# An expert's weights in one transfer instead of two, in a mixture-of-experts stage on one core

## The chip, the core and the metric

The kernel runs on one core of one Trainium2 chip. The metric is the time on the device in microseconds (us), from one execution to the next the median of three. A core has five engines with a queue of instructions each: TensorE (PE, with its weight loads shown apart as PEld), VectorE (DVE), ScalarE (ACT), GpSimd (POOL) and SyncE (SP), which here does nothing but start transfers. Transfers run on 16 DMA engines, and say by a semaphore that they have landed.

## What is computed

Two layers, each of a cross attention and a feed-forward part, on 800 tokens of width 1024. The change lies in the feed-forward part of layer 0, a mixture of 32 experts of which each token takes four:

```python
logits = x @ gate_w.T + gate_b
topk_logits, topk_idx = jax.lax.top_k(logits, 4)
topk_weight = softmax(topk_logits)
# rows sorted by expert (xt, gid: the expert of each row), then for each expert:
gate = xt @ w_gate[e] + b_gate[e]            # w_gate[e], w_up[e]: 1024 x 512
up   = xt @ w_up[e]   + b_up[e]
gate = minimum(gate, 7.0); up = clip(up, -7.0, 7.0)
activated = (up + 1.0) * gate * sigmoid(1.702 * gate)
outs = activated @ w_down[e] + b_down[e]     # w_down[e]: 512 x 1024
y = sum over the token's four experts of outs * topk_weight
```

All weights are float32. One expert has 4 MB of gate and up weights (1024 x 1024 numbers) and 2 MB of down weights (512 x 1024 numbers), 6 MB in all, beside a small bias row.

## The kernel before, in words

The stages run one after the other: attention 0, the mixture (`moe`), attention 1, a ternary feed-forward part. Each engine has its own program, and semaphores tie them.

**Blocks and steps.** The router counts how many rows each expert gets and rounds them up to blocks of 64 rows (`BS`). With the inputs of this kernel there are 67 blocks (the router's counts follow from the inputs). The list of blocks, in the order of the experts, is cut into three queues of 23 (`NQ_W` is 3), and the stage takes a block of each queue in turn, so that step `s` works on queue `s % 3`. A loop of 12 passes over six steps gives 72 steps.

**Weights.** SBUF holds three places for an expert's weights, one for each queue: `W2[:, q, :]`, of which the first `W2_D` = 8192 numbers of a partition are gate and up and the other 4096 are down, and `bias3[:, q, :]`. An expert stays in its place while its queue has blocks of it. When a queue goes on to its next expert, the place is loaded anew. There are 34 loads (`N_LOADS`): one for each queue at the start, and 31 in a loop on SP. The router's tables tell this loop, for load `i`, the expert, the place, and how many steps must be done before the place is free (`load_i`, rows 0, 1 and 2). By L1230 that last number is the first step of the new expert less two: the place is free when the step three before the first use is over, since that was the last one of its queue.

**One step of TensorE** (`one` in `moe_tensor`, L1467). It reads the table `need_g` for the number of loads that must have landed, waits for the semaphore `m_wg`, and runs the first half of the gate and up matmuls of step `s` (L1442), the transposes of the next tile of rows (`turn`, L1434) and of the activations of step `s - 1` (`turn_act`, L1450), the second half of gate and up, which signals `m_gu`, and last the down matmuls of step `s - 1` (`down`, L1463), which signal `m_y`. So the down part of a step is over only at the end of the step behind it. `down` reads a table of its own, `need_d`, and waits for a semaphore of its own, `m_wd`.

**One load on SP** (`moe_sync`, L1359 to L1373). Wait until the load before has landed (`m_wg`), and until the gate and up matmuls of the last step that used the place are over (`m_gu`): start the 4 MB of gate and up (L1365). Wait for that step's activations (`m_act`): start the two bias transfers (L1368), which count on `m_wg` too. Wait until the down part of the load before has landed (`m_wd`) and the last down matmuls of the place are over (`m_y`): start the 2 MB of down (L1372). SP works through this in order.

**The rest.** POOL gathers the next 128 rows of tokens into the one buffer `hs` (L1394), one gather for two steps, as soon as TensorE has transposed the rows before (`m_tp`). ACT empties the transposes and the results and starts the stores of the results `ysb` (L1554) from a queue of its own. DVE applies the activation (L1494 to L1502). The router's own buffers lie where the weights of places 1 and 2 will be: `pt` in the gate and up part of place 2, `pl` in the down part of place 2, which is in use until the last gate weights are in (`m_gk`).

Of the kernel before, what the change touches and what calls it, by code (L numbers as in the profile page):

```python
# [9 lines left out]
I32 = mybir.dt.int32  # L10
U32 = mybir.dt.uint32
ALU = mybir.AluOpType
# [4 lines left out]
P = 128  # L17
# [3 lines left out]
E, TOPK, FI = 32, 4, 512  # L21
# [19 lines left out]
G = 2  # L41
# [12 lines left out]
MAX_STEPS = IT * MAX_IT  # L54
# [1 line left out]
MIN_TILES = MIN_IT * TPI  # L56
FILL = -(-(MAX_TILES - MIN_TILES) // HG)
N_LOADS = E + NQ_W - 1
GU_INC, DN_INC = 16 * (1 + G), 16
assert MAX_STEPS <= P and N_LOADS <= P and T <= BS * MIN_BLOCKS // NQ_W  # L60
EC = FE // P
NBLK = 2
# [14 lines left out]
W2_D = KC * 2 * FI  # L77
W2_N = W2_D + IC * D
# [76 lines left out]
def build(nc, A, stages=("a0", "moe", "a1", "ffn")):  # L155
    ctx = ExitStack()
    with ctx:
        sems = {}

        def sem(name):  # L160
            if name not in sems:
                sems[name] = ctx.enter_context(nc.semaphore(name))
            return sems[name]
# [6 lines left out]
        PS = ctx.enter_context(nc.psum_tensor("PS", [P, 8, 512], F32))  # L170
# [85 lines left out]
        idxc = [pm.put(f"idxc{i}", [P, 1], I32) for i in range(TPI)]  # L256
        np_i = pm.put("np_i", [P, 4], I32)
        need_g = pm.put("need_g", [P, MAX_STEPS], I32)
        need_d = pm.put("need_d", [P, MAX_STEPS], I32)
        first_e = pm.put("first_e", [P, NQ_W], I32)  # L260
        load_i = pm.put("load_i", [P, 3, N_LOADS], I32)

# [867 lines left out]
        def route_vector(dve):  # L1130
# [113 lines left out]
            dve.sem_inc(sem("m_te"), 1)  # L1244
            dve.wait_ge(sem("m_tet"), 1)
            ts(need_g[0:1, :], PS[0:1, 1, 0:MAX_STEPS], float(GU_INC), float(GU_INC), ALU.mult, ALU.add)
            ts(need_d[0:1, :], PS[0:1, 1, 0:MAX_STEPS], float(DN_INC), float(DN_INC), ALU.mult, ALU.add)
            for k in range(3):
                vt.tensor_copy(load_i[0:1, k, :], PS[0:1, 1, (k + 1) * P:(k + 1) * P + N_LOADS])
            link(dve, ts(np_i[0:1, 0:1], rounds[0:1, :], 1.0, None, ALU.add))  # L1250
# [68 lines left out]

        def moe_sync(sp):  # L1320

            def load_gate_up(e, q):
                sp.dma_start(W2[:, q, 0:W2_D], A["W2"][e, :, 0:W2_D]).then_inc(sem("m_wg"), 16)

            def load_bias(e, q):
                for g in range(G):
                    sp.dma_start(bias3[g * BS:(g + 1) * BS, q, :],
                                 A["b2"][e, g:g + 1, :].to_broadcast([BS, N1])).then_inc(sem("m_wg"), 16)

            def load_down(e, q):  # L1330
                sp.dma_start(W2[:, q, W2_D:W2_N], A["W2"][e, :, W2_D:W2_N]).then_inc(sem("m_wd"), 16)

            sp.wait_ge(sem("a_qc"), 16 * HG)
            sp.wait_ge(sem("m_fill"), 16 * HG)
            load_gate_up(0, 0)
            load_down(0, 0)
            sp.wait_ge(sem("a_folded"), 2)
            sp.dma_start(gwT[:, :, :], A["gwT"].rearrange("p (c e) -> p c e", c=KC)).then_inc(sem("m_gw"), 16)
            sp.dma_start(gb[:, :], A["gb"].to_broadcast([P, E])).then_inc(sem("m_gw"), 16)
            sp.dma_start(bd, A["bd"]).then_inc(sem("m_gw"), 16)  # L1340
            load_bias(0, 0)
            for m in range(MT):
                sp.wait_ge(sem("ln_hn"), ln_count("moe", "hn", m + 1))
                sp.dma_start(h_d[m * P:(m + 1) * P, :], HN["moe"][m % 2][:, :]).then_inc(sem(f"moe_st{m % 2}"), 16)
            sp.wait_ge(sem("m_first"), 1)
            sp.wait_ge(sem("moe_st0"), 16 * ((MT + 1) // 2))
            sp.wait_ge(sem("moe_st1"), 16 * (MT // 2))
            for q in range(1, NQ_W):
                if q == 2:
                    sp.wait_ge(sem("m_tab"), 1)  # L1350
                e = sp.value_load(first_e[0:1, q:q + 1], min_val=0, max_val=E - 1)
                sp.wait_ge(sem("m_wg"), GU_INC * q)
                load_gate_up(e, q)
                load_bias(e, q)
                if q == 2:
                    sp.wait_ge(sem("m_gk"), TOPK)
                sp.wait_ge(sem("m_wd"), DN_INC * q)
                load_down(e, q)
            with sp.Fori(NQ_W, N_LOADS) as i:  # L1359
                e = sp.value_load(load_i[0:1, 0, bass.ds(i, 1)], min_val=0, max_val=E - 1)  # L1360
                q = sp.value_load(load_i[0:1, 1, bass.ds(i, 1)], min_val=0, max_val=NQ_W - 1)
                done = sp.value_load(load_i[0:1, 2, bass.ds(i, 1)], min_val=1, max_val=MAX_STEPS)
                sp.wait_ge(sem("m_wg"), GU_INC * i)
                sp.wait_ge(sem("m_gu"), done)
                sp.dma_start(W2[:, bass.ds(q, 1), 0:W2_D].rearrange("p a n -> p (a n)"), A["W2"][e, :, 0:W2_D]).then_inc(sem("m_wg"), 16)  # L1365
                sp.wait_ge(sem("m_act"), done)
                for g in range(G):
                    sp.dma_start(bias3[g * BS:(g + 1) * BS, bass.ds(q, 1), :].rearrange("p a n -> p (a n)"),  # L1368
                                 A["b2"][e, g:g + 1, :].to_broadcast([BS, N1])).then_inc(sem("m_wg"), 16)
                sp.wait_ge(sem("m_wd"), DN_INC * i)  # L1370
                sp.wait_ge(sem("m_y"), done)
                sp.dma_start(W2[:, bass.ds(q, 1), W2_D:W2_N].rearrange("p a n -> p (a n)"),  # L1372
                             A["W2"][e, :, W2_D:W2_N]).then_inc(sem("m_wd"), 16)  # L1373

        def iterations(eng, one):

# [49 lines left out]
        def moe_tensor(pe):  # L1426
            def turn(t, k, part):
                if part == 0:
                    pe.wait_ge(sem("m_hs"), 16 * t + 16)
                if not (isinstance(t, int) and t == 0):  # L1430
                    pe.wait_ge(sem("m_tpe"), 2 * t - 1 + part)
                for c in range(4):
                    cc = 4 * part + c
                    mm = nc.tensor.transpose(PS[:, 6 + part, c * P:(c + 1) * P], hs[:, cc * P:(cc + 1) * P], ident)  # L1434
                mm.then_inc(sem("m_tp"), 1)

            def gate_up(s, u, cs):
                k, half, q = u // G, u % G, u % NQ_W
                for c in cs:
                    for g in range(G):  # L1440
                        o = c * 2 * FI + g * N1
                        mm = nc.tensor.matmul(PS[g * BS:(g + 1) * BS, 2 + u % 2, :], hT2[k][:, c, half * BS:(half + 1) * BS],  # L1442
                                              W2[:, q, o:o + N1], start=c == 0, stop=c == KC - 1)
                if cs[-1] == KC - 1:
                    mm.then_inc(sem("m_gu"), 1)

            def turn_act(s):
                pe.wait_ge(sem("m_act"), s + 1)
                for j in range(FH // P):
                    mm = nc.tensor.transpose(PS[:, 0, j * P:(j + 1) * P], act[:, j * P:(j + 1) * P], ident)  # L1450
                mm.then_inc(sem("m_at"), 1)

            def down(s, u, spare=1):
                ready = pe.value_load(need_d[0:1, bass.ds(s, 1)], min_val=DN_INC, max_val=DN_INC * N_LOADS)
                pe.wait_ge(sem("m_wd"), ready)
                pe.wait_ge(sem("m_ate"), s + 1)
                if not (isinstance(s, int) and s < 2):
                    pe.wait_ge(sem("m_ye"), s - spare if spare else s)
                for c in range(IC):
                    g, j = c // (FH // P), c % (FH // P)  # L1460
                    for h in range(G):
                        o = W2_D + c * D + h * DH
                        mm = nc.tensor.matmul(PS[h * BS:(h + 1) * BS, 4 + u % 2, :], actT[:, j, g * BS:(g + 1) * BS],  # L1463
                                              W2[:, u % NQ_W, o:o + DH], start=c == 0, stop=c == IC - 1)
                mm.then_inc(sem("m_y"), 1)

            def one(it, u):  # L1467
                s, t = it * IT + u, it * TPI + u // G
                head = isinstance(it, int) and it == 0
                ready = pe.value_load(need_g[0:1, bass.ds(s, 1)], min_val=GU_INC, max_val=GU_INC * N_LOADS)  # L1470
                pe.wait_ge(sem("m_wg"), ready)
                pe.wait_ge(sem("m_tpe"), 2 * t + 1)
                if not (head and u < 2):
                    pe.wait_ge(sem("m_act"), s - 1)
                gate_up(s, u, range(0, KC // 2))
                turn(t + 1, (u // G + 1) % TPI, u % G)
                if not (head and u == 0):
                    turn_act(s - 1)
                pe.wait_ge(sem("m_tpe"), 2 * t + 2)
                gate_up(s, u, range(KC // 2, KC))  # L1480
                if not (head and u == 0):
                    down(s - 1, (u - 1) % IT)

            for part in range(2):
                turn(0, 0, part)
            last = iterations(pe, one)
            turn_act(last)
            down(last, IT - 1, spare=0)
# [458 lines left out]
```

## Time and profile before

| | |
|---|---|
| median of three runs | 4007.51 us (4003.28 to 4011.58) |
| the profiled execution | 4008.97 us |
| its span, first to last instruction | 4007.3 us |
| busy: PE / PEld / DVE / ACT / POOL | 92 / 45 / 47 / 21 / 19% |
| mean granted TensorE clock | 0.961 |
| the 72 steps of the mixture | 1425 to 2306 us of the span |
| DMA in these 881 us | busy share 0.71, 276 GB/s |

Times of instructions are counted from the start of the span. The profiled execution has 1.7 us around its span. The page's groups name an instruction by line, engine and operation. A transfer's "landing" is the time from its issue to its semaphore. The granted clock is 1.00 at TensorE's full 2.4 GHz and 0.50 at 1.2 GHz.

### The profile page before, as it was taken

Reading aid. Unit: us, or ns where it says so; the run is one execution under the profiler, and the core shown is the slowest. Engines: PE = TensorE matmul, PEld = TensorE weight load, DVE = VectorE, ACT = ScalarE, POOL = GpSimd, SP = SyncE. Lnnn points to the kernel's source line nnn. Section 1 sums busy time; section 2 is a strip of 40 time slices with the busy share of each in tenths; the row PEclk is TensorE's granted clock in tenths of the full one; section 3 lists DMA queues with packets and bytes.
Section 4 is the critical chain, followed back from the end, with each engine's and each line's share of the span. In section 5 each row is a group of like instructions: output and inputs, shape, how many; then the busy total and the mean of one; then the engine's idle time right before and its main releaser. Section 6 shows DMA issues by size and latency. Waiting matters only on the chain.

```text
span 4007.3 us, 39516 instructions
## 1 busy us (share of the span) xinstructions
PE 3669.5 (92%) x14286; PEld 1807.1 (45%) x14287; DVE 1896.9 (47%) x1697; ACT 843.3 (21%) x1406; POOL 759.1 (19%) x620
## 2 busy tenths in 40 slices
PE   7899999999999699999999839999999999899999
PEld 4454454455455333333333325545455454454554
DVE  7784484475476521111111155618447175662561
ACT  1220131131032111111111114324143151220110
POOL 5500400400310100000000020000000010792780
PEclk9999999999999789999999969999999999999999
DMA  5621121121122375787779374335144150330330
GB/s 189 219 108 55 56 110 44 67 103 48 54 84 87 118 307 202 289 339 306 265 271 361 124 275 158 116 108 179 70 158 140 54 178 24 116 136 32 110 110 33
DMA packets 96135, 581.50 MB, mean 145 GB/s; under 512 B 12264, under 2 KB 12392, under 8 KB 82080
## 3 DMA queue, kind: packets, MB, share of 16 engines
q1 hardware_dynamic: 55120, 449.80, 29.7%
q0 software_dynamic: 24976, 90.34, 6.9%
q10 hardware_dynamic: 15936, 39.86, 2.8%
q8 instruction: 81, 1.33, 0.1%
q14 instruction: 22, 0.18, 0.0%
HBM read 533.16 MB, written 46.79 MB: 145 GB/s over the span
## 4 chain that ended last, share of the span: by engine, by line
PE 73%; DVE 9%; DMA 6%; issue 5%; POOL 5%; ACT 1%; SPq 0%; ACTq 0%; DVEq 0%; POOLq 0%
PE PS L748 11%; PE PS L1442 11%; PE PS L734 11%; PE PS L868 8%; PE PS L1463 6%; PE PS L1790 4%; POOL gtq L1709 4%; PE PS L623 3%; DMA hs<-h_d,idxc 3%; PE PS L638 2%; PE PS L714 2%; DMA stg<-in_F 2%; PE PS L858 2%; DVE mx L1033 2%; PE PS L1763 1%
## 5 line engine op out<-in xcount | busy, mean ns | idle before, releaser
L734 PE MATMUL PS<-qc,kvT 128*128 128x400 f32 x1536 | 542.3, 505 | 9.7 <-ACT qc L893 4.8
L1442 PE MATMUL PS<-W,hT 128*64 128x512 f32 x2304 | 536.9, 609 | 0.0
L748 PE MATMUL PS<-Sb,kvN 128*128 128x400 f32 (+1 forms) x1536 | 534.0, 504 | 2.5 <-DVE qc L1049 2.5
L1033 DVE TENSOR_REDUCE mx<-Sb 128x400 f32<-128x2400 f32 x64 | 274.4, 4287 | 288.5 <-ACT Sb L973 288.5
L748 PEld LDWEIGHTS PS<-Sb,kvN 128*128 128x128 f32 (+1 forms) x1536 | 295.3, 192 | 234.2 <-issue 15.8
L734 PEld LDWEIGHTS PS<-qc,kvT 128*128 128x128 f32 x1536 | 288.9, 192 | 222.6 <-issue 21.2
L1494 DVE TENSOR_TENSOR gu<-PS,bias 128x512 f32<-128x512 f32 x72 | 49.8, 692 | 712.6 <-PE PS L1442 712.6
L1763 PE MATMUL PS<-xh,wq 128*128 128x400 f16 x2048 | 353.8, 334 | 18.8 <-DVE wq L1639 18.0
L1093 POOL TENSOR_TENSOR qrope<-rt,rt 128x400 f32<-128x400 f32 x192 | 206.9, 1100 | 828.0 <-DVE rt L1010 828.0
L868 PE MATMUL PS<-wb,ctxl 128*128 128x512 f32 x768 | 331.7, 593 | 4.7 <-ACT ctxl L893 4.7
L1709 POOL TENSOR_SCALAR gtq<-stg,thr 128x1024 f16<-128x1024 f32 x96 | 310.4, 3246 | 114.3 <-DMA stg<-in_F 114.0
L1442 PEld LDWEIGHTS PS<-W,hT 128*64 128x64 f32 x2304 | 162.4, 140 | 312.1 <-issue 310.1
L1763 PEld LDWEIGHTS PS<-xh,wq 128*128 128x128 f16 x2048 | 198.9, 98 | 173.7 <-issue 20.8
L1463 PE MATMUL PS<-W,actT 128*64 128x512 f32 x1152 | 264.0, 601 | 6.8 <-ACT actT L1539 4.1
L1042 DVE TENSOR_REDUCE sums<-Sb 128x400 f32<-128x2400 f32 x64 | 266.0, 4156 | 0.0
L1010 DVE TENSOR_TENSOR rt<-PS,ropeq 128x800 f32<-128x800 f32 x192 | 180.8, 984 | 166.0 <-PE PS L638 165.2
L973 ACT ACTIVATE Sb<-PS 128x400 f32<-128x400 f32 x320 | 159.2, 503 | 413.1 <-PE PS L734 413.1
L1029 DVE TENSOR_TENSOR Sb<-Sb,PS 128x2400 f32<-128x2400 f32 x64 | 169.9, 2655 | 159.9 <-PE PS L842 159.9
L868 PEld LDWEIGHTS PS<-wb,ctxl 128*128 128x128 f32 x768 | 145.3, 190 | 189.7 <-issue 179.9
L1063 DVE TENSOR_TENSOR X<-PS,X 128x512 f32<-128x512 f32 x96 | 66.4, 691 | 305.3 <-PE PS L868 305.3
L1639 DVE SCALAR_TENSOR_TENSOR wq<-stg,nthr,gtq 128x1024 f16<-128x1024 f32 x64 | 141.8, 2254 | 111.0 <-POOL gtq L1709 111.0
L982 ACT ACTIVATE Sb<-Sb 128x2400 f32<-128x2400 f32 x64 | 141.1, 2205 | 239.1 <-DVE Sb L1029 239.1
(246 smaller groups left out, 3604.8 us busy)
## 6 DMA issues: line engine op xcount, KB each, us to landing
W<-in_W SPq DMA_DIRECT2D x34, 4096.0 KB, 13.0
W<-in_W SPq DMA_DIRECT2D x34, 2048.0 KB, 8.0
kvT<-kvT_d SPq DMA_DIRECT2D x64, 768.0 KB, 5.8
kvN<-kvN_d SPq DMA_DIRECT2D x64, 768.0 KB, 4.4
stg<-in_F SPq DMA_DIRECT2D x32, 1536.0 KB, 6.5
absin<-in_F POOLq DMA_DIRECT2D x48, 512.0 KB, 4.0
hn<-in_F POOLq DMA_DIRECT2D x48, 512.0 KB, 3.8
wb<-in_WB SPq DMA_DIRECT2D x8, 2560.0 KB, 10.3
```

The costliest lines, as they stand in the source:

```text
L734: mm = nc.tensor.matmul(PS[:, lc % 3, 0:GW], kvT[b % 2][:, dc, lc * P:(lc + 1) * P], qc[:, dc, b, :], start=dc == 0, stop=dc == CC - 1)
L748: mm = nc.tensor.matmul(PS[:, 6 + dc, 0:GW], kvN[b % 3][0:k, lc, dc * P:(dc + 1) * P], Sb[b % 3][0:k, lc, :], start=lc == 0, stop=lc == LC ...
L868: mm = nc.tensor.matmul(PS[:, 2 + n % 4, :], ctxl[:, a, m * P:(m + 1) * P], wb[:, w:w + 512], start=a == 0, stop=a == HA - 1)
L1010: ins = nc.vector.tensor_tensor(rt[k % 2][j][:, :, :].rearrange("p i (b s) -> p i b s", b=BH), src, tab, ALU.mult)
L1029: nc.vector.tensor_tensor(sb, sb, PS[:, 4, 0:GW].unsqueeze(1).to_broadcast([P, LC, GW]), ALU.add).then_inc(sem(f"{p}_sb"), 1)
L1033: nc.vector.tensor_reduce(mx[:, :], Sb[st % 3][:, :, :].rearrange("p c n -> p n c"), AX, ALU.max).then_inc(sem(f"{p}_mx"), 1)
L1042: nc.vector.tensor_reduce(sums[:, :], Sb[(st - 1) % 3][:, :, :].rearrange("p c n -> p n c"), AX, ALU.add).then_inc(sem(f"{p}_sum"), 1)
L1093: ins = nc.gpsimd.tensor_tensor(qrope[k % 4][:, i, :], rt[k % 2][0][:, i, :], rt[k % 2][1][:, 1 - i, :], ALU.add)
L1442: mm = nc.tensor.matmul(PS[g * BS:(g + 1) * BS, 2 + u % 2, :], hT2[k][:, c, half * BS:(half + 1) * BS], W2[:, q, o:o + N1], start=c == 0, ...
L1463: mm = nc.tensor.matmul(PS[h * BS:(h + 1) * BS, 4 + u % 2, :], actT[:, j, g * BS:(g + 1) * BS], W2[:, u % NQ_W, o:o + DH], start=c == 0, s ...
L1709: nc.gpsimd.tensor_scalar(gtq[q][:, w, :], stg[q][:, w, :], thr[:, w:w + 1], None, ALU.is_gt).then_inc(sem("f_gt"), 1)
L1763: mm = nc.tensor.matmul(PS[:, 4 * q + 2 * w + half, 0:HALF], wq[q][:, w, c, :], xh[part][:, c, half * HALF:(half + 1) * HALF], start=c == ...
```

## The change

Gate, up and down of an expert are loaded by one transfer of 128 rows of 12288 numbers (6 MB). The semaphore `m_wd` and the table `need_d` are gone, and with them TensorE's second wait in a step. The one transfer starts when the whole place is free, that is on `m_y`; the two bias transfers start right behind it. The waits for `m_gu` and `m_act` on SP are gone. At the start, the load of place 2 also waits for `m_gk`.

```diff
-GU_INC, DN_INC = 16 * (1 + G), 16
+GU_INC = 16 * (1 + G)
...
-            ts(need_d[0:1, :], PS[0:1, 1, 0:MAX_STEPS], float(DN_INC), float(DN_INC), ALU.mult, ALU.add)
...
-            def load_gate_up(e, q):
-                sp.dma_start(W2[:, q, 0:W2_D], A["W2"][e, :, 0:W2_D]).then_inc(sem("m_wg"), 16)
+            def load_weights(e, q):
+                sp.dma_start(W2[:, q, :], A["W2"][e]).then_inc(sem("m_wg"), 16)
...
-            def load_down(e, q):
-                sp.dma_start(W2[:, q, W2_D:W2_N], A["W2"][e, :, W2_D:W2_N]).then_inc(sem("m_wd"), 16)
...
-            load_gate_up(0, 0)
-            load_down(0, 0)
+            load_weights(0, 0)
...
             for q in range(1, NQ_W):
                 if q == 2:
                     sp.wait_ge(sem("m_tab"), 1)
+                    sp.wait_ge(sem("m_gk"), TOPK)
                 e = sp.value_load(first_e[0:1, q:q + 1], min_val=0, max_val=E - 1)
                 sp.wait_ge(sem("m_wg"), GU_INC * q)
-                load_gate_up(e, q)
+                load_weights(e, q)
                 load_bias(e, q)
-                if q == 2:
-                    sp.wait_ge(sem("m_gk"), TOPK)
-                sp.wait_ge(sem("m_wd"), DN_INC * q)
-                load_down(e, q)
             with sp.Fori(NQ_W, N_LOADS) as i:
...
                 sp.wait_ge(sem("m_wg"), GU_INC * i)
-                sp.wait_ge(sem("m_gu"), done)
-                sp.dma_start(W2[:, bass.ds(q, 1), 0:W2_D].rearrange("p a n -> p (a n)"), A["W2"][e, :, 0:W2_D]).then_inc(sem("m_wg"), 16)
-                sp.wait_ge(sem("m_act"), done)
+                sp.wait_ge(sem("m_y"), done)
+                sp.dma_start(W2[:, bass.ds(q, 1), :].rearrange("p a n -> p (a n)"), A["W2"][e]).then_inc(sem("m_wg"), 16)
                 for g in range(G):
                     sp.dma_start(bias3[g * BS:(g + 1) * BS, bass.ds(q, 1), :].rearrange("p a n -> p (a n)"),
                                  A["b2"][e, g:g + 1, :].to_broadcast([BS, N1])).then_inc(sem("m_wg"), 16)
-                sp.wait_ge(sem("m_wd"), DN_INC * i)
-                sp.wait_ge(sem("m_y"), done)
-                sp.dma_start(W2[:, bass.ds(q, 1), W2_D:W2_N].rearrange("p a n -> p (a n)"),
-                             A["W2"][e, :, W2_D:W2_N]).then_inc(sem("m_wd"), 16)
...
             def down(s, u, spare=1):
-                ready = pe.value_load(need_d[0:1, bass.ds(s, 1)], min_val=DN_INC, max_val=DN_INC * N_LOADS)
-                pe.wait_ge(sem("m_wd"), ready)
                 pe.wait_ge(sem("m_ate"), s + 1)
```

On SP, the body of the loop over loads 3 to 33, before (names: `W_48704_109` are the three places of weights, `bias_196160_110` the three bias places):

```order
183  L1365 ISA [waits m_gu,m_wg]
184  L1365 DMA W_48704_109<-in_W 128x8192
185  L1368 ISA [waits m_act]
186  L1368 DMA bias_196160_110<-in_b 64x512
187  L1368 ISA
188  L1368 DMA bias_196160_110<-in_b 64x512
189  L1370 REGISTER_ALU
190  L1372 ISA [waits m_y,m_wd]
191  L1372 DMA W_48704_109<-in_W 128x4096
```

and the same body of the changed kernel, whose lines have other numbers:

```order
178  L1356 ISA [waits m_y,m_wg]
179  L1356 DMA W_48704_109<-in_W 128x12288
180  L1358 ISA
181  L1358 DMA bias_196160_110<-in_b 64x512
182  L1358 ISA
183  L1358 DMA bias_196160_110<-in_b 64x512
```

Nothing is issued ahead of the wait for `m_y` any more: gate and up have moved from ahead of it to behind it.

On TensorE, the start of the down matmuls of one step, before (`actT_117` are the transposed activations):

```order
946  L1454 TENSOR_LOAD need_d_127
947  L1454 ISA x2
948  L1463 MATMUL PS<-W_48704_109,actT_117 64x512 [waits m_ye,m_ate,m_wd]
949  L1463 MATMUL PS<-W_48704_109,actT_117 64x512 x7
```

and in the changed kernel:

```order
942  L1447 MATMUL PS<-W_48704_109,actT_117 64x512 [waits m_ye,m_ate]
943  L1447 MATMUL PS<-W_48704_109,actT_117 64x512 x7
```

The table's load and the wait for `m_wd` are gone; the matmuls and their order are the same.

## Rows read from the trace of the kernel before

**Rows 1.** Busy time by stretch: the 72 steps (us, busy and count by engine, PEclk, DMA, GB/s).

```profile
1425.00:2306.00 881.00, 835.99 (x3890) 296.29 (x3890) 148.97 (x369) 135.59 (x290) 41.08 (x72) 0.97 0.71 276
```

**Rows 2.** Waits of PE and PEld in 1425 to 2310 (us in total, times, longest).

```profile
PE PS L1434 <- DMA hs<-h_d,idxc: 38.2, 9, 6.2
...
PEld PS L1442 <- DMA bias<-in_b: 2.0, 7, 0.3
...
PEld PS L1463 <- DMA W<-in_W: 0.6, 2, 0.3
```

**Rows 3.** Timeline of PE over one undisturbed step (start, duration, line and operation).

```profile
1644.16 3.60 PE L1442 MATMUL PS<-W,hT 128*64 128x512 f32 x16
...
1648.50 3.65 PE L1442 MATMUL PS<-W,hT 128*64 128x512 f32 x16
1651.98 3.60 PE L1463 MATMUL PS<-W,actT 128*64 128x512 f32 x16
1655.42 3.60 PE L1442 MATMUL PS<-W,hT 128*64 128x512 f32 x16
```

**Rows 4.** Timeline of SP: a single load, and two loads for steps in succession.

```profile
1629.91 0.36 SPq L1365 DMA_DIRECT2D W<-in_W  x1
...
1644.59 0.35 SPq L1372 DMA_DIRECT2D W<-in_W  x1
...
1689.62 0.34 SPq L1372 DMA_DIRECT2D W<-in_W  x1
1692.58 0.36 SPq L1365 DMA_DIRECT2D W<-in_W  x1
...
1700.87 0.34 SPq L1372 DMA_DIRECT2D W<-in_W  x1
```

**Rows 5.** The bias transfers of SP in 1689 to 1694.5.

```profile
L1368 SPq DMA_DIRECT2D bias<-in_b x2: 492/517/542, 1693.1 to 1693.9; - x2
DMA to landing us min/median/max: 14.9/15.1/15.2
```

**Rows 6.** The same for SP in 1604 to 1609, the weights' issues first.

```profile
L1372 SPq DMA_DIRECT2D W<-in_W x1: 345/345/345, 1604.1 to 1604.1; - x1
...
L1368 SPq DMA_DIRECT2D bias<-in_b x2: 491/512/533, 1607.6 to 1608.3; - x2
DMA to landing us min/median/max: 16.5/16.6/16.6
```

**Rows 7.** The weights' transfers of SP in 1372 to 1376, load 1.

```profile
L1323 SPq DMA_DIRECT2D W<-in_W x1: 376/376/376, 1373.0 to 1373.0; - x1
L1331 SPq DMA_DIRECT2D W<-in_W x1: 446/446/446, 1374.9 to 1374.9; - x1
DMA to landing us min/median/max: 12.3/14.4/16.5
```

**Rows 8.** Line L1365, the 31 gate and up transfers, and line L1372, the 31 down transfers.

```profile
L1365 SPq DMA_DIRECT2D W<-in_W x31: 350/353/356, 1436.4 to 2211.8; - x31
...
DMA to landing us min/median/max: 12.5/13.0/16.8
...
DMA to landing us min/median/max: 7.5/8.0/18.4
```

**Rows 9.** Timeline of PE around two waits for gathered rows.

```profile
1614.92 3.60 PE L1442 MATMUL PS<-W,hT 128*64 128x512 f32 x16
1623.57 1.11 PE L1434 MATMUL PS<-cst,hs 128*128 128x128 f32 x4 [5.04 <-DMA hs<-h_d,idxc]
...
1632.91 3.60 PE L1442 MATMUL PS<-W,hT 128*64 128x512 f32 x16
...
1711.69 3.60 PE L1442 MATMUL PS<-W,hT 128*64 128x512 f32 x16
1720.20 1.11 PE L1434 MATMUL PS<-cst,hs 128*128 128x128 f32 x4 [4.90 <-DMA hs<-h_d,idxc]
...
1730.71 3.60 PE L1442 MATMUL PS<-W,hT 128*64 128x512 f32 x16
```

**Rows 10.** Busy time by stretch, right behind the second of these waits.

```profile
1720.20:1726.00 5.80, 5.80 (x18) 2.39 (x20) 0.00 (x0) 1.47 (x3) 0.00 (x0) 0.50 0.96 358
```

**Rows 11.** The gathers of POOL, L1394, in 1425 to 2306.

```profile
DMA to landing us min/median/max: 4.2/7.2/15.6
```

More of the change, by code:

```diff
@@ L258, in build @@
         need_g = pm.put("need_g", [P, MAX_STEPS], I32)
-        need_d = pm.put("need_d", [P, MAX_STEPS], I32)
         first_e = pm.put("first_e", [P, NQ_W], I32)
```

## The prediction

> **What bounds the kernel now.** I read the page's busy shares first, then the busy time of the stretch in which the experts are worked on, then the waits of TensorE in it, then its timeline and SP's side by side. The change touches only this stretch of 72 steps. There TensorE is busy for 836 of 881 us at a mean granted clock of 0.97 [rows 1], so the stage is TensorE's. The waits say how well the weights are hidden: TensorE lost 2.0 us in seven waits for a bias and 0.6 us in two for weights, but 38.2 us in nine waits for gathered rows `hs` [rows 2]. So no weight transfer costs anything today, and any time by which one comes late is new time at the end.
>
> An undisturbed step has the period 1655.42 - 1644.16 = 11.26 us [rows 3]: both halves of gate and up, the transposes, and the down matmuls of the step before. The next step starts where the down matmuls end.
>
> Beside it SP: a single load starts its 4 MB at 1629.91, during a step, as soon as the gate and up matmuls of the place's last step are over, and its 2 MB at 1644.59, once the down matmuls are over as well [rows 4]. The latter is 0.43 us behind the start of the step at 1644.16 [rows 3]. Two facts follow. SP needs 0.43 us from the end of the down matmuls to the issue. And the 4 MB are issued 14.7 us ahead of the moment at which the whole place is free.
>
> **The slack, before and after.** The step that needs a place is the third after the last one that used it. Its gate and up matmuls stand at the head of the step, so the 4 MB have about 3.4 us of down matmuls of the last-use step and two whole steps: some 26 us, against landings of 12.5 to 16.8 us [rows 8]. The 2 MB start a step later and are needed by the down matmuls, which for that block stand at the end of the step behind its own: two steps and most of a third, some 30 us, against 7.5 to 18.4 us [rows 8]. After the change everything waits for `m_y` of the last use. That comes at the end of the step behind the last use, and just one step, 11.26 us, lies between it and the first gate and up matmul of the new expert. The whole 6 MB and the bias, which SP issues behind it and which counts on the same semaphore, must land in this step.
>
> **The cost of one transfer.** No row shows 6 MB in one piece, but some loads follow each other so closely that 2 MB, 4 MB and the bias queue one behind the other. From the issue at 1689.62 [rows 4] to the last bias, 1693.9 + 15.1 [rows 5], are 19.4 us. From 1604.1 to 1608.3 + 16.6 [rows 6] are 20.8 us; in this one a gather of rows fell in as well. The low end is load 1, when nothing else moved: issues at 1373.0 and 1374.9, the second landed at 1374.9 + 16.5, with the bias between them, 18.4 us in all [rows 7]. I take 19.8 us, between the two that run beside steps and a little nearer to the first, as only one step in two gathers. The ends are 18.4 and 20.8.
>
> By the Trainium skill, "DMA: Bandwidth & Descriptors", section "Anatomy of one DMA — SWDGE (gpsimd) path", a transfer costs about 2.0 us fixed and then its bytes at 436 GB/s. By this, as an estimate of that page's figures, 6 MB would take 16.4 us, and two transfers in a row 18.4 us: merging would save 2 us. The trace has 12.5 us [rows 8] at best for the 4 MB, where this gives 11.6. If it held here, each of the late transfers below would be about 3 us shorter. That is one of the rivals.
>
> **New waits.** One load: 0.43 + 19.8 - 11.26 = 9.0 us in which TensorE stands at the head of a step. Queued behind the waiting matmul are the whole step, its transposes, and the down matmuls of the step before, so ACT, DVE and POOL stand too, and nothing overtakes. All 31 loads of the loop are needed at once at their first step, so there are 31 such waits (the count is that of [rows 8]). A load whose neighbour is for the step right before can't begin before that one has landed; it then has the same one step to hide in, and costs the same 9.0 us. 31 x 9.0 = 279 us.
>
> **The clock behind a wait.** A stop of some 5 us can be seen twice [rows 9]: the step with the 5.04 us wait takes 17.99 us, which is 1.69 more than period and wait; the one with the 4.90 us wait takes 19.02 us, 2.86 more. Behind the second the granted clock is 0.50 (1.2 GHz) for 5.8 us [rows 10]. I take 2.3 us for each restart, the mean, with 1.7 and 3.4 us (a step's half slowed by all of 6.8 us) as ends. A restart costs only where the next step isn't itself waiting for a transfer that already flies: in pairs like the one at 1689.62 and 1700.87 [rows 4], issues of L1372 one step apart, the transfer for the second step covers the slow step. I count 11 such among the 31, which leaves 20 restarts: 20 x 2.3 = 46 us.
>
> **What goes.** The nine waits for `hs` came from gathers that shared the queues with weights: such a gather landed after up to 15.6 us, one alone after 4.2 [rows 11], and it has about one step. After the change a weight transfer fills the step before its use and the wait at the head of the next; the gather issued beside it is needed 3.5 us behind that wait, when the transfer is over. So I let all nine go: 38.2 us and nine restarts at 2.3 us, 59 us. If they stay, this term is 0.
>
> **Costed at nothing.** TensorE's load of `need_d` and its wait: the steps show matmul behind matmul [rows 3], so nothing is exposed. The router's one instruction less, on DVE, is under 1 us. The wait for `m_gk` at the start moves the load of place 2 by some 27 us, to about 1428; it then lands near 1447, about when step 2 starts. I put this at 0, with up to 3 us if the transfer is contended. SP's shorter list is hidden, as SP waits.
>
> **Sum.** 279 + 46 - 59 = +266 us. The profiled execution took 4008.97 us, 1.7 us more than its span, and lies 1.5 us above the median of the runs; 4009 + 266 = 4275 us. That is 6.6% slower.
>
> **Rivals.**
> - *The gathers still wait.* Each of the DMA engines has fewer and longer weight pieces now, and the gather's small ones must get between them. By the Trainium skill, same page, section "Queues, rings and completion order", an engine takes turns between queues at the grain of a packet, so a longer packet would hold the gather up for longer. No row here shows a piece of 48 KB. What speaks for it is the landing of 15.6 us; against it, the order of events above. Time: 4275 + 59 = 4334 us.
> - *One transfer is cheaper than two.* A transfer of 16.9 us instead of 19.8 (the 18.4 of [rows 7], less another 1.5 for the second issue and its bias in between) leaves waits of 6.1 us: 31 x 2.9 = 90 us less, 4185 us. Against it: the queues were already full without a break in the two close pairs [rows 5, 6].
> - *Not slower.* The waits for gathers go and the transfer fits into the step. The kernel would take 4009 - 59 = 3950 us. It decides at the length of the transfer at which 31 waits (each 0.43 + length - 11.26) cost 59 us: 12.7 us. The 4 MB alone take 12.5 [rows 8], so 6 MB can't, unless the loop's count of finished steps were met one step earlier than I read it from L1230.
> - *The change doesn't do what it says* (the transfer is split, or the bias lands much later): included in the range's upper part.
>
> **Chances.** The forecast 0.80, gathers still waiting 0.08, a cheaper transfer 0.09, not slower 0.03. The forecast's own range: a transfer of 18.4 us takes off 31 x 1.4 = 43 us, one of 20.8 adds 31; restarts at 1.7 or 3.4 us are -12 or +22 us on 20 of them; half of the gather waits staying is +30. Together about 4215 to 4330 us. Reached out a little towards the cheaper transfer, 4205 to 4335. A measurement of this kernel can tell about 0.2% from no change, which is 8 us. Faster by more than that: 0.02; within it: 0.01; slower: 0.97.
>
> **What would show it.** In the profile after: TensorE's waits name the bias or the weights before L1442's successor, about 31 of some 9 us (6 us in the second of a pair, where the step before ran slow), in all 240 to 280 us; waits for `hs` nearly gone; the stretch of the steps near 1147 us instead of 881, with a clock below 0.97; the weights' transfer landing after 17 to 19 us and the last bias 19 to 20.5 us behind the issue; SP's issue 0.4 us behind the head of a step. The prediction is wrong if the weights are issued before the end of the down matmuls of the step behind the last use, if the waits are under 6 us each, or if the stages before 1425 and behind the last step change their length.

## The result, and the profile after

The changed kernel is slower, as forecast: 4249.8 us in the median of four runs (4244.6 to 4254.8) against 4009.6 (4003.3 to 4011.8), a ratio of 1.060 with a 95% interval of 1.058 to 1.062. That is 240 us more, where 266 had been forecast. The profiled execution took 4244.62 us, its span 4242.9.

The stretch of the 72 steps holds all of it. The busy times by stretch (columns as in [rows 1]) are, of the changed kernel:

```profile
1425.00:2550.00 1125.00, 884.30 (x3886) 300.99 (x3884) 147.37 (x364) 134.50 (x288) 41.07 (x71) 0.89 0.56 220
```

The stretch is 1125 us long instead of 881 [rows 1], 244 more. TensorE is busy 48 us longer with the same matmuls, since its mean clock fell from 0.97 to 0.89; the other 196 us it stands still. The DMA engines are idle more often than before (share 0.56 against 0.71) although each wait is a wait for them. Weights that are on their way in only part of the time can't be limited by bandwidth as a whole: they start late.

Who waits, of the changed kernel in 1425 to 2570 (us in total, times, longest; compare [rows 2]):

```profile
PE PS L1428 <- DMA bias<-in_b: 235.0, 32, 9.9
...
PE PS L1420 <- DMA hs<-h_d,idxc: 1.6, 1, 1.6
```

L1428 is the gate and up matmul (L1442 before). 31 waits of the loop's loads, 232 us, and one of 2.8 us at the start have appeared, and the 38.2 us for gathered rows have shrunk to 1.6. Weights and bias are waited for together, and the bias lands last, so it gets the name.

How one wait comes about is best read on SP and TensorE side by side. TensorE of the changed kernel (start, duration, line, operation, wait ahead in brackets):

```profile
1892.21 3.60 PE L1428 MATMUL PS<-W,hT 128*64 128x512 f32 x16
...
1900.03 3.60 PE L1447 MATMUL PS<-W,actT 128*64 128x512 f32 x16
1911.46 6.43 PE L1428 MATMUL PS<-W,hT 128*64 128x512 f32 x16 [7.83 <-DMA bias<-in_b]
```

and SP at the same time:

```profile
1892.65 0.35 SPq L1356 DMA_DIRECT2D W<-in_W  x1
1893.23 1.24 SPq L1358 DMA_DIRECT2D bias<-in_b  x2
```

The 6 MB are issued 0.44 us into the step that starts at 1892.21. Their landing, and that of the bias:

```profile
L1356 SPq DMA_DIRECT2D W<-in_W x1: 355/355/355, 1892.7 to 1892.7; - x1
...
DMA to landing us min/median/max: 17.6/17.6/17.6
...
L1358 SPq DMA_DIRECT2D bias<-in_b x2: 497/514/532, 1893.2 to 1894.0; - x2
...
DMA to landing us min/median/max: 17.4/17.5/17.5
```

The last bias lands at 1894.0 + 17.5 = 1911.5, 18.8 us behind the issue of the weights, and the next step starts there. The step that covers the load, 11.26 us long, is over at 1903.5. Over all 31 loads of the loop the weights land in

```profile
DMA to landing us min/median/max: 17.5/17.7/18.8
```

What the stop does to the clock is in the stretch right behind that wait (1911.5) and in two behind another wait, of 7.76 us (1866.7, then 1872.7):

```profile
1866.70:1872.70 6.00, 6.00 (x16) 1.83 (x16) 0.00 (x0) 0.00 (x0) 0.00 (x0) 0.50 0.19 44
1911.50:1917.10 5.60, 5.60 (x14) 1.68 (x16) 0.00 (x0) 0.00 (x0) 0.00 (x0) 0.50 0.20 47
1872.70:1877.00 4.30, 4.30 (x24) 1.70 (x22) 0.00 (x0) 0.87 (x2) 0.00 (x0) 1.00 0.00 0
```

TensorE is fully busy in each, but does 16 matmul records in 6.0 us at 0.50 (1.2 GHz), and 24, of which a quarter are short transposes, in 4.3 us once it is back at 1.00. The 16 matmuls of half a gate and up part took 6.64 us behind this wait and 3.65 us in the second half of the same step:

```profile
1866.66 6.64 PE L1428 MATMUL PS<-W,hT 128*64 128x512 f32 x16 [7.76 <-DMA bias<-in_b]
...
1874.04 3.65 PE L1428 MATMUL PS<-W,hT 128*64 128x512 f32 x16
```

Not all of the 244 us reaches the span of the profiled execution, which is 236 us longer. Behind the stage the profiled executions differ by 8 us the other way (1701 us before, 1693 after), in attention 1, whose code is the same. Most of it is one kind of wait, before:

```profile
PE PS L686 <- issue: 13.1, 2, 6.7
```

and after:

```profile
PE PS L685 <- issue: 5.5, 1, 5.5
```

It came up twice in one execution and once in the other. The kernels of the experiments have the same attention 1, and their profiles have the wait too: 0, 0, 0, 5.3 and 7.0 us of it where the weights of the mixture start late, as in the changed kernel, and 5.7, 11.8 and 11.8 us where they start early. What starts it isn't known here, and with one profile of each kernel it can neither be counted as an effect of the change nor ruled out as one.

### The profile page after: what moved, and what is told of

It reads as the page before. It is cut to its first block, busy times and chain, and to the rows that moved or that the text cites. A ratio compares the mean times of both kernels' runs of the same rounds, so it can differ in the third digit from the quotient of the medians.

```text
span 4242.9 us, 39057 instructions
## 1 busy us (share of the span) xinstructions
PE 3718.7 (88%) x14286; PEld 1811.9 (43%) x14287; DVE 1895.3 (45%) x1696; ACT 843.5 (20%) x1406; POOL 759.1 (18%) x620
## 4 chain that ended last, share of the span: by engine, by line
PE 63%; DMA 17%; DVE 8%; POOL 5%; issue 5%; SPq 1%; ACT 1%; ACTq 0%; DVEq 0%; POOLq 0%
DMA bias<-in_b 14%; PE PS L747 11%; PE PS L733 11%; PE PS L867 8%; PE PS L1428 8%; PE PS L1774 4%; POOL gtq L1693 4%; PE PS L622 3%; PE PS L1447 3%; PE PS L637 3%; DMA stg<-in_F 2%; PE PS L713 2%; PE PS L857 2%; DVE mx L1032 2%; PE PS L649 1%
## 5 line engine op out<-in xcount | busy, mean ns | idle before, releaser
L1428 PE MATMUL PS<-W,hT 128*64 128x512 f32 x2304 | 590.2, 660 | 235.0 <-DMA bias<-in_b 235.0
L1428 PEld LDWEIGHTS PS<-W,hT 128*64 128x64 f32 x2304 | 172.6, 151 | 592.9 <-issue 432.3
L1747 PE MATMUL PS<-xh,wq 128*128 128x400 f16 x2048 | 353.9, 334 | 19.3 <-DVE wq L1623 18.4
## 6 DMA issues: line engine op xcount, KB each, us to landing
W<-in_W SPq DMA_DIRECT2D x34, 6144.0 KB, 17.7
```

The costliest lines, as they stand in the source:

```text
L1747: mm = nc.tensor.matmul(PS[:, 4 * q + 2 * w + half, 0:HALF], wq[q][:, w, c, :], xh[part][:, c, half * HALF:(half + 1) * HALF], start=c == ...
```

## The experiments

Eight kernels. Each time is a median of four runs (five for `e8_pieces_2mb`). The kernel before was timed beside them: 4003.4 us for e1, e3, e4 and e5, and 4007.3 for e2, e6, e7 and e8. Ratios are to that kernel and have their 95% interval. Differences from the changed kernel are differences of medians. Taken by the ratios' own base, the kernel before as it ran beside each, they come out up to 6 us otherwise: e3's 172 us as 166, e6's 40 as 37, e2's 19 as 16, and e7's 16 as 18.

**The late start of gate and up alone** (`e1_late_two`).

```diff
                 sp.wait_ge(sem("m_wg"), GU_INC * i)
-                sp.wait_ge(sem("m_gu"), done)
+                sp.wait_ge(sem("m_y"), done)
                 sp.dma_start(W2[..., 0:W2_D] ...).then_inc(sem("m_wg"), 16)
```

> The kernel before with one edit: gate and up (4 MB) of the loop's loads wait for m_y as well, and down (2 MB) stays a transfer of its own with its own semaphore. Theory (the late start costs): 4 MB and bias take about 13.8 us from an issue 0.43 us into a step of 11.26, so 20 waits of 3.1 us and 11 of some 6 us where the 2 MB of the load before are still in the queue, 128 us, restarts of the clock some 34, half of the gather waits gone, 30: about 4140 us. Rival (the merging itself costs, by longer pieces or by one semaphore for all): nothing is merged here, so about 4010 us.

Measured: 4128.7 us, ratio 1.032 (1.030 to 1.033). The waits of TensorE in its profile:

```profile
PE PS L1442 <- DMA bias<-in_b: 124.3, 31, 6.6
...
PE PS L1434 <- DMA hs<-h_d,idxc: 0.9, 1, 0.9
```

The expected 128 us of waits are there as 124, in 31 waits. Nothing is merged in this kernel, so about 125 of the 240 us come from the start of the 4 MB alone. Half of the gather waits had been expected to stay; 0.9 us did. So they go with the late start, and merging isn't needed for it.

**Half the change the other way: one semaphore, early start kept** (`e5_one_sem`).

```diff
-GU_INC, DN_INC = 16 * (1 + G), 16
+GU_INC = 16 * (2 + G)
...
-                sp.wait_ge(sem("m_wd"), DN_INC * i)
                 sp.wait_ge(sem("m_y"), done)
-                sp.dma_start(W2[..., W2_D:W2_N] ...).then_inc(sem("m_wd"), 16)
+                sp.dma_start(W2[..., W2_D:W2_N] ...).then_inc(sem("m_wg"), 16)
...
-                ready = pe.value_load(need_d[0:1, bass.ds(s, 1)], min_val=DN_INC, max_val=DN_INC * N_LOADS)
-                pe.wait_ge(sem("m_wd"), ready)
```

> The kernel before with the other half of the change alone: three transfers as before, gate and up started early on m_gu, but all on m_wg with one table, so that the first matmul of an expert waits for its down weights too, and a load starts only when the one before has landed whole. Theory (the late start of the 4 MB costs, the shared semaphore only where loads follow each other): single loads have 2 MB and 8 us in a step of 11.26 and are hidden; in the 11 pairs the second's down lands some 5 to 6 us late: +60 us, some gather waits less, about 4050 us. Rival (waiting for all three at once is what costs): close to 4250 us. Rival (it costs nothing): 4009 us.

Measured: 4038.7 us, ratio 1.009 (1.007 to 1.011). TensorE's waits in 1420 to 2400:

```profile
PE PS L1438 <- DMA W<-in_W: 67.6, 11, 7.6
...
PE PS L1430 <- DMA hs<-h_d,idxc: 4.0, 2, 2.5
```

Exactly 11 waits, at 6.1 us each, for the weights: the eleven loads whose neighbour is for the step right before. The other 20 loads cost nothing, because 2 MB fit into a step. The shared semaphore thus costs 35 us while the large part still starts early, net of the gather waits that went. The two halves of the change, each by itself, cost 125 and 35 us. The other 80 of the 240 come only when both are there: 2 MB more must then land in the one step of cover, for each of the 31 loads.

**Less to carry behind the same start** (`e3_4mb`). The changed kernel, whose loop loads only gate and up.

```diff
-                sp.dma_start(W2[:, bass.ds(q, 1), :].rearrange("p a n -> p (a n)"), A["W2"][e]).then_inc(sem("m_wg"), 16)
+                sp.dma_start(W2[:, bass.ds(q, 1), 0:W2_D].rearrange("p a n -> p (a n)"), A["W2"][e, :, 0:W2_D]).then_inc(sem("m_wg"), 16)
```

> The changed kernel, but the loads of the loop bring only the 4 MB of gate and up; the down weights of the loop's experts are left out (those of the first three are used on). Theory (the wait is issue plus length of the transfer less one step): the transfer and bias end 5.1 us earlier, 13.8 us behind the issue, waits of some 3 us instead of 7 to 9, restarts cheaper by about 1 us each: about 4070 us. Rival (each stop costs a fixed amount whatever the size, by the order of the semaphores): about 4250 us, as the changed kernel.

Measured: 4077.5 us, ratio 1.019 (1.017 to 1.021). In its profile:

```profile
PE PS L1428 <- DMA bias<-in_b: 89.2, 29, 4.9
```

The weights land after 12.8 us in the median, 4.9 less than 6 MB. Each wait is 3.1 us. This kernel leaves out the loop's down weights, so its results are not those of the reference. Against the changed kernel, 172 us are saved over 31 loads, 5.6 us each: the length of the missing 2 MB and a little of the restart.

**An earlier `m_y`** (`e6_down_early`), in the changed kernel:

```diff
-                gate_up(s, u, range(KC // 2, KC))
+                gate_up(s, u, range(KC // 2, KC // 2 + 1))
                 if not (head and u == 0):
                     down(s - 1, (u - 1) % IT)
+                gate_up(s, u, range(KC // 2 + 1, KC))
```

> The changed kernel, but in each step the down matmuls of the step before stand behind five eighths of the gate and up matmuls instead of behind all of them, so that m_y comes 2.7 us earlier, with the same work. Theory (the wait is set by when m_y lets the transfer start): the 20 loads without a neighbour right before start 2.7 us earlier and their waits are as much shorter; the 11 others start when the load before has landed and gain nothing: 54 us less, about 4196 us. Rival (the transfers are bound by the DMA queues all along): 4250 us. Rival (all 31 gain): 84 us less, 4166 us.

Measured: 4210.1 us, ratio 1.051 (1.048 to 1.053), 40 us below the changed kernel where 54 were expected. The waits:

```profile
PE PS L1428 <- DMA bias<-in_b: 184.0, 32, 7.2
```

They are 51 us shorter. A single load that waited 7.8 us now waits 5.1, 2.7 less, as its start moved 2.7 us forward. That the time fell by less stands in the stretch of the steps, of the changed kernel and of this one:

```profile
1424.10:2550.80 1126.70, 885.90 (x3889) 301.29 (x3888) 148.24 (x367) 135.09 (x289) 41.26 (x72) 0.89 0.56 220
1428.50:2519.30 1090.80, 901.12 (x3889) 302.02 (x3888) 148.22 (x367) 131.57 (x289) 41.25 (x72) 0.89 0.58 227
```

The stretch is 36 us shorter and not 51, because TensorE is busy 15 us longer with as many matmuls. Its mean clock is 0.89 in both, although it stands still less: more of its work falls into slow stretches.

**The bias ahead of the weights** (`e2_bias_first`), in the changed kernel:

```diff
+                sp.wait_ge(sem("m_act"), done)
+                (the two bias transfers, moved up)
                 sp.wait_ge(sem("m_y"), done)
                 sp.dma_start(W2[:, bass.ds(q, 1), :] ..., A["W2"][e]).then_inc(sem("m_wg"), 16)
-                (the two bias transfers)
```

> The changed kernel, but each load's two bias transfers start ahead of the weights, as soon as the activations of the place's last use are there, not behind the weights. Theory: the step waits for the last byte of the load; in the changed kernel the weights land 17.7 us behind their issue and the bias 1.2 us after them. With the bias out of the way each of the 31 waits is about 1.2 us shorter, 37 us in all: about 4213 us, and the waits name the weights. Rival (the weights alone hold the step, the bias runs beside them): no difference, 4250 us.

Measured: 4231.1 us, ratio 1.056 (1.054 to 1.059), 19 us less, half of what was expected.

```profile
PE PS L1429 <- DMA W<-in_W: 214.2, 31, 9.2
```

The waits now name the weights. Single loads without a gather beside them gained 0.9 us (7.8 to 6.9), those with one some 1.6 (9.4 to 7.8), and the 20 single ones 23 us in all, about the 1.2 us each that were expected. Where the load before has only just landed, SP must issue the two biases, 1.2 us, before it can start the weights; these 11 waits grew by 5 us in all. That had been overlooked.

**The one transfer in six pieces** (`e7_after_pieces`), in the changed kernel:

```diff
-                sp.dma_start(W2[:, bass.ds(q, 1), :] ..., A["W2"][e]).then_inc(sem("m_wg"), 16)
+                for o in range(0, W2_N, PC):
+                    sp.dma_start(W2[:, bass.ds(q, 1), o:o + PC] ..., A["W2"][e, :, o:o + PC]).then_inc(sem("m_wg"), 16)
```

`PC` is 2048 numbers, 8 KB of a partition; the three loads at the start are cut in the same way.

> The changed kernel, with its one 6 MB transfer cut into six of 1 MB (8 KB rows), all issued at the same point and on the same semaphore. Theory (when the weights start is what costs, not that they are one transfer): within 15 us of 4250 us, the last bias landing about as long behind the first issue as now, 18.9 us. Rival (a single transfer with 48 KB rows is slow or holds others up): under 4220 us.

Measured: 4265.9 us, ratio 1.065 (1.062 to 1.067), 16 us above the changed kernel, just past the 15 given. Waits of 245.4 us instead of 235.0. One transfer is slightly better than six when all start at one point: what is gained by merging as such is real, and small against what the start costs. The rival (long rows are slow, under 4220 us) is refuted.

**The kernel before, in pieces** (`e4_pieces` with 1 MB, `e8_pieces_2mb` with 2 MB). Here the question was the other term of the forecast, the waits for gathered rows.

```diff
-                sp.dma_start(W2[:, bass.ds(q, 1), 0:W2_D] ..., A["W2"][e, :, 0:W2_D]).then_inc(sem("m_wg"), 16)
+                for o in range(0, W2_D, PC):
+                    sp.dma_start(W2[:, bass.ds(q, 1), o:o + PC] ..., A["W2"][e, :, o:o + PC]).then_inc(sem("m_wg"), 16)
```

and the same for down; `PC` is 2048 or 4096 numbers, rows of 8 or 16 KB instead of 32 and 16.

> The kernel before, with each weight transfer cut into 1 MB transfers (8 KB rows): four for gate and up, two for down, same waits, same semaphores with larger counts. Theory (the nine gather waits of 38 us come from the gather's small pieces taking turns with 32 KB rows of weights): the gathers land sooner, their waits and the restarts behind them go, 4009 - 59 = 3950 us, less what SP's longer list costs. Rival (the gathers wait for bandwidth, which is the same): 4009 us, with waits for hs near 38 us.

> The kernel before with weight transfers of 2 MB (16 KB rows): two for gate and up, one for down. The version with 1 MB transfers had waits for gathered rows of 2.3 us instead of 38.2. Theory (gather pieces take turns with rows of weights, so the row's length sets the delay): with rows of half the length before, waits for hs of 0 to 20 us, time 3975 to 3990 us. Rival (it was the number of transfers or another order that helped, with no grading by row length): 4003 us, or all of the gain.

Measured: 3974.6 us, ratio 0.993 (0.991 to 0.995), with 1 MB, and 3976.6 us, ratio 0.993 (0.991 to 0.995), with 2 MB. Both beat both kernels. It is 29 and 31 us less than the kernel before, half of the 59 that had been expected of the first. The waits with 1 MB:

```profile
PE PS L1447 <- DMA bias<-in_b: 18.1, 4, 7.0
...
PE PS L1439 <- DMA hs<-h_d,idxc: 2.3, 2, 1.3
```

and with 2 MB:

```profile
PE PS L1439 <- DMA hs<-h_d,idxc: 19.7, 12, 2.1
...
PE PS L1447 <- DMA bias<-in_b: 5.7, 3, 2.6
```

The waits for `hs` are 38.2, 19.7 and 2.3 us with rows of 32, 16 and 8 KB, and the longest landing of a gather is 15.6 [rows 11], 11.6 and 10.6 us. The landings, with 2 MB and then with 1 MB:

```profile
DMA to landing us min/median/max: 4.2/7.1/11.6
...
DMA to landing us min/median/max: 4.0/7.5/10.6
```

The median landing did not move (7.2 before). What got shorter are the gathers that share the engines with weights all the way, and those had the waits. The version with 1 MB waits 18.1 us for biases instead, mostly at the third of three loads in a row. In the profiled executions the stage, from its first gate and up matmul to its last down matmul, takes 881.3 us before, 855.4 with 2 MB and 846.8 with 1 MB, so it too grades with the row's length, by less than the waits for `hs`. The whole time does not: behind the stage the profile with 2 MB is 7 us shorter than the other two, with one wait of 5.7 us in attention 1 where the one with 1 MB has 11.8. The first rival of the expectation for 1 MB (the gathers wait for bandwidth) is refuted.

More transfers and shorter rows came together in these kernels, so the times alone don't tell which of the two helped. The transfers' own view does (packets, MB, and the share of the 16 engines' time in a stretch). q1 is the queue of SP, q0 that of the gather; the queue of the stores is left out. In the kernel before (1614 to 1620), in the changed kernel (2162.7 to 2169.7) and with 1 MB transfers (1754.4 to 1757.4):

```profile
q1 hardware_dynamic: 70, 2.29, 88.4%
q0 software_dynamic: 67, 0.27, 11.1%
...
q1 hardware_dynamic: 63, 3.10, 102.1%
q0 software_dynamic: 60, 0.25, 8.5%
...
q1 hardware_dynamic: 102, 0.81, 65.9%
q0 software_dynamic: 100, 0.41, 34.0%
```

Each time there are about as many rows of the gather as rows of weights, while a row of weights has 32, 48 or 8 KB. So the engines take one row from either queue in turn, and an engine gets to a gather's row every 1.4 us, 1.9 us or 0.5 us (16 engines times the stretch, over the rows). A gather has 128 rows, eight for each of 16 engines.

This is what the Trainium skill says in "DMA: Bandwidth & Descriptors", section "Queues, rings and completion order": an engine takes turns between its queues packet by packet. The trace agrees, with one row as the turn: in the median one 32 KB row of weights occupies an engine for 1.21 us, a 16 KB row for 0.61, an 8 KB row for 0.31 and a 48 KB row of the changed kernel for 1.82. The kernels that start late show it too: with rows of 48 KB the longest landing of a gather is 15.2 us, with the same 6 MB in rows of 8 KB (`e7_after_pieces`) it is 9.6.

## Why the prediction was right

**Where the wait comes from: right.** The issue 0.43 us behind the head of the step before (0.44 measured), one step of cover, 31 waits, named after the bias. e1 and e3 changed the start and the size apart, and e6 the start by 2.7 us, and the waits followed each.

**The length of the transfer: the mis-sized term.** 19.8 us were taken from the issue to the last bias. Single loads without a gather beside them mostly show 18.6 to 18.9, those with one 20.0 to 20.6, and the mean of all 31 is 19.3. From the starts of the 72 steps in the trace, the mean from the head of the covering step to the head of the one that waited is 19.73 us, for the 20 single loads and for the 11 seconds of a pair alike. The forecast was 0.43 + 19.8 = 20.23. Half a microsecond too much, 31 times, is 15.5 us. The two close pairs that stood for the transfer, 19.4 us without a gather and 20.8 with one, were each some 0.6 us longer than what they stood for. Why isn't shown. For the same reason the waits of the 31 loads sum to 232 us and not to the 240 to 280 that had been named.

**The restarts: right, and a little too high.** In the 20 steps with a wait ahead and none behind, the excess over 11.26 us is 2.1 us on average (1.4 to 3.0); 2.3 had been taken. 20 x 0.2 = 4 us.

**What goes: right.** Over the 71 steps before, the excess over 11.26 us was 59.5 us in sum; 59 had been put down for nine waits and restarts. Of it, one wait of 1.6 us stayed. The gathers are not faster where weights fly (landings up to 15.2 us in the changed kernel, beside 15.6 [rows 11]). They are needed later: behind the wait for the weights.

**Costed at nothing.** The wait of place 2 for `m_gk` did cost: its load, issued at 1426.88, held step 2 up by 2.8 us, inside the 3 us allowed. The slow matmuls behind that wait cost nothing more, as the load for step 3 was in flight beside them.

**Sum.** 31 x (19.73 - 11.26) = 263, + 20 x 2.1 = 42, - 59.5, + 3 at the start: 248 us. The head of the last step moved by 247 us against that of the first. The first step began 1.6 us earlier and the last matmuls took 1.4 us less, which leaves the 244 of the stretch.

**The range** held the result, but its upper end was added up otherwise than its lower: the parts named give 4275 - 43 - 12 = 4220 below and 4275 + 31 + 22 + 30 = 4358 above, where 4335 had been put down. One of its own signs of being wrong did come up, too: the stages behind the last step changed their length, by 8 us. Whether the change did that stays open (the wait in attention 1, above).

**The rivals.** Cheaper by 3 us a load: it had the last bias 16.9 us behind the issue, and it never came before 18.5. e7 shows that six transfers in place of the one cost 16 us in all, half a microsecond a load. By the Trainium skill, "DMA: Bandwidth & Descriptors", section "Anatomy of one DMA — SWDGE (gpsimd) path", 6 MB would take 16.4 us, as an estimate from its figures. The 6 MB took 17.7 us in the median and 17.5 at best, on SP's queue, so this estimate was 1.3 and 1.1 us short. Gathers still waiting: refuted by the 1.6 us above. The turn-taking on which it rested is there, but the weights have landed when the gathered rows are needed. Not slower: 6 MB would have had to land, bias included, in 12.7 us. The nearest trial is e3, where 4 MB and the bias end 14.4 us behind the issue in the mean; it is already slower, by 1.9%.

## What to carry to other kernels

A merged transfer starts when the last of its parts may start and is awaited when the first of them is needed. Before merging, write down for each part the time from "its place is free" to "it is needed": here 26 us for 4 MB and 30 us for 2 MB became 11 us for 6 MB. The cost is then the number of loads times what sticks out, plus about 2 us for TensorE's clock each time that it stood still (4 to 10 us here) and runs on.

When a small transfer must get through beside large ones, shorten the rows of the large ones. Two or four transfers for the 4 MB, with the same start, took the waits for gathered rows from 38 to 20 and 2 us. Both kernels are 0.7% faster than the one before; the shortest rows gained no more of the whole time than the middle ones.

## What the runs showed of the hardware

A row of 48 KB in each partition is moved as one piece: 1.82 us on an engine, 27 GB/s, nearly the same rate as rows of 32, 16 and 8 KB (1.21, 0.61 and 0.31 us). The rate doesn't speak for the long row, and the turn-taking speaks against it: a gather beside such rows got one of its own through every 1.9 us, beside 8 KB rows every 0.5 us.

A bias row spread to 64 partitions, 128 KB, ends about 1.2 us behind 6 MB of weights on the same queue (17.6 and 18.8 us behind the issue of the weights). Issued ahead of them, as in e2, it lands in 2.9 us in the median, but SP spends 1.2 us on the issue of the two.
